# Adding the experts' rows to the nodes: accumulating scatters and per-tile combining in a two-layer graph network on one Trainium2 core

## What is computed

```python
x = x + L0_gnn(layernorm(x), src, dst, ...)      # attention over edges, then a dense FFN
x = x + L0_ffn(layernorm(x), gate_w, gate_b, w1, b1, w2, b2)
x = x + L1_gnn(layernorm(x), edge_attr_4, edge_attr_8, src, dst, ...)
x = x + L1_ffn(layernorm(x), ...)

# L0_ffn: top-2 of 8 experts, at most cap = int(1.2 * T / 8) = 187 rows per expert
topw, topi = top_k(softmax(xf @ gate_w.T + gate_b), 2)
w_te = einsum('tk,tke->te', topw, one_hot(topi)); wm = where(routed, w_te, -1)
sel_w, sel_idx = top_k(wm.T, cap)
h = gelu(xf[sel_idx] @ w1 + b1); out = h @ w2 + b2            # 512 -> 2048 -> 512
of = zeros.at[sel_idx].add(out * sel_w)

# L1_ffn: a shared FFN plus two banks ("sp", "fq") of 8 experts, top-1 each
y = gelu(x2 @ Ws1 + bs1) @ Ws2 + bs2
for bank in (sp, fq):
    slot, gate = route(x2, Wr, br)                            # capacity is never reached here
    y = y + gate * (gelu(buf @ W1 + b1) @ W2 + b2)[slot]      # 512 -> 256 -> 512
```

## Time and profile before

| | |
|---|---|
| median of 3 runs | 1875.65 us (1869.82 to 1876.59) |
| the profiled execution | 1875.17 us |
| its span in the trace | 1873.4 us |
| PE busy | 1594.3 us, 85% |
| DVE, ACT, POOL busy | 959.7, 701.4, 559.6 us |
| mean granted TensorE clock | 0.925 of 2.4 GHz |
| `experts0` / preparation in `messages` / `experts1` | 863 to 1211 us / 1216 to 1267 us / 1699 us to the end |

### The profile page before, as it was taken

How to read it: one execution, slowest core, us unless ns; L and a number is a source line. 1 busy time by engine, 2 the same in 40 slices (tenths; PEclk the granted TensorE clock), 3 DMA queues, 4 the chain that set the end, 5 groups by cost and what they waited for, 6 DMA issues and landing times. The chain is left out here.

```text
span 1873.4 us, 31644 instructions
## 1 busy us (share of the span) xinstructions
PE 1594.3 (85%) x9860; PEld 1167.9 (62%) x9860; DVE 959.7 (51%) x1950; ACT 701.4 (37%) x1610; POOL 559.6 (30%) x638
## 2 busy tenths in 40 slices
PE   1993077999999797897999999858999999898994
PEld 0551045888888455555999999844555555655662
DVE  8330098766766386361000000168999999542233
ACT  0230055555555133443211112154555555441331
POOL 6777601101010121151000000046555555133133
PEclk6997588999999898798999999968999999998997
DMA  9900011011000600557566552075555555619985
GB/s 290 312 11 6 6 43 23 13 23 22 12 11 1 149 12 1 220 142 249 198 229 238 218 196 99 18 216 165 156 158 158 156 156 150 215 37 287 353 268 183
DMA packets 131143, 252.87 MB, mean 135 GB/s; under 512 B 35344, under 2 KB 52596, under 8 KB 126572
## 3 DMA queue, kind: packets, MB, share of 16 engines
q1 hardware_dynamic: 91692, 171.81, 27.6%
q0 software_dynamic: 39360, 79.86, 14.6%
HBM read 196.03 MB, written 55.52 MB: 134 GB/s over the span
## 5 line engine op out<-in xcount | busy, mean ns | idle before, releaser
L1998 PE MATMUL acc<-prod,ohy 128*64 128x256 f32 x1056 | 249.1, 386 | 7.3 <-DVE prod L2116 7.3
L2042 ACT ACTIVATE ohy<-oh,RECS 128x64 f32<-128x64 f32 x704 | 187.0, 336 | 151.6 <-PE acc L1998 151.6
L1998 PEld LDWEIGHTS acc<-prod,ohy 128*64 128x64 f32 x1056 | 138.4, 138 | 131.9 <-issue 69.5
L1975 POOL DMA_INDIRECT rows<-up_dram,idx x176 | 167.0, 949 | 144.3 <-DVE prod L2116 101.2
L272 POOL DMA_INDIRECT rec_dram<-recs,pos x157 | 160.4, 1022 | 59.9 <-issue 48.9
L2001 PE MATMUL acc<-prod,ohy 128*64 128x256 f32 x704 | 177.3, 395 | 0.0
L1752 DVE TENSOR_SCALAR FT<-y_ps,b2T 128x188 f32<-128x188 f32 x32 | 13.2, 413 | 319.2 <-PE y_ps L1701 319.2
L1689 PE MATMUL hid_ps<-FT,W 128*128 128x188 f32 x1024 | 168.1, 326 | 0.7 <-ACT FT L1726 0.7
L2116 DVE TENSOR_TENSOR prod<-w_ps,rows 128x768 f32<-128x768 f32 x176 | 166.3, 945 | 0.0
L1689 PEld LDWEIGHTS hid_ps<-FT,W 128*128 128x128 f32 x1024 | 165.6, 192 | 0.9 <-issue 0.9
L1701 PE MATMUL y_ps<-hid,W 128*128 128x188 f32 x1024 | 164.5, 323 | 0.0
(11 more groups left out here) (380 smaller groups left out, 2638.2 us busy)
## 6 DMA issues: line engine op xcount, KB each, us to landing
W<-in_L_ffn_w SPq DMA_DIRECT2D x16, 4096.0 KB, 15.9
bankW_sp<-in_L_ffn_W_sp SPq DMA_DIRECT2D x2, 4096.0 KB, 23.9
xin<-zeros SPq DMA_DIRECT2D x31, 256.0 KB
h_dram<-h3e SPq DMA_DIRECT2D x22, 256.0 KB, 4.8
h<-h_dram SPq DMA_DIRECT2D x22, 256.0 KB
QF<-q_dram SPq DMA_DIRECT2D x20, 250.0 KB, 4.1
xin_sp<-zeros SPq DMA_DIRECT2D x17, 256.0 KB
xin_fq<-zeros SPq DMA_DIRECT2D x17, 256.0 KB
```

The lines of the kernel that those rows point to most:

```text
L1975: pool.indirect_dma_start(out=rows[:, t, :], out_offset=None, in_=up_dram, in_offset=bass.IndirectOffsetOnAxis(ap=idx[:, par, t:t + 1], ax ...
L1998: upper = lambda m: nc.tensor.matmul(acc[0:HALFB, bank, :].rearrange("p (b c) -> p b c", c=MUL)[:, m:4:3 - m, :], ohs[:, 1 + m, :], pr[:, ...
L2042: last = nc.scalar.activation(ohy[:, t % OHY, i, :], oh[:, par, t, :], ACT.Copy, scale=RECS[:, bass.ds(BATCH * g + t, 1), 4 + i])
```

## The change

**First expert layer.** `X` is stored to a DRAM buffer `x_dense` during `place_choices` (20 DMAs by SP, between its stores of the hidden layer). The rows of `xin0` are 8 elements wider (520 instead of 512) and carry the two weights, the two expert numbers and the node number; unused rows carry a node number from 1250 up, behind the real nodes. In `experts0` DVE reads the number and the weight from the loaded rows, multiplies the transposed result by the weight on its way to `ye`, and POOL adds each half of 94 rows into `x_dense` with an accumulating indirect scatter; each waits until the one before has landed. `yout0`, `slot_out`, `weight` and the 20 gathers are gone: `send_rows` loads `X` back from `x_dense` with 20 plain DMAs on SP, and DVE starts from there. The clearing of 12 blocks of `MSG` moves from ACT to POOL.

**Second expert layer.** The rows of `xin_sp` and `xin_fq` are wider in the same way. At the end of `tail` SP stores `X` to `x_shared` (20 DMAs). In `experts1` every row tile is combined by itself: POOL gathers the 128 nodes' running rows (`x_shared` for the first bank, `x_first` for the second) into a ring of 5, DVE adds the gated result, POOL scatters them on (to `x_first`, or to the output). A gather waits until the scatter five tiles before has landed, the first gather of the second bank until all of the first bank's scatters have. The final gathers, adds and stores are gone. `ye` is a ring of 4 instead of 3.

```diff
-        X = sb("X", [P, TILES, DIM])
+        X128 = sb("X", [128, TILES, DIM])
+        X = X128[0:P]
...
                         for b in range(ECHUNKS):
                             store_hidden(sp, b)
+                            if b < TILES:
+                                for p0, p1 in TILE_PARTS:
+                                    sp.dma_start(x_dense[P * b + p0:P * b + p1, :], X[p0:p1, b, :]).then_inc(x_stored, 16)
...
+                        for e in range(EXPERTS):
+                            b = e % 2
+                            pool.wait_ge(noted, 2 * (e + 1))
+                            for c in range(2):
+                                pool.wait_ge(back_moved, 2 * e + c + 3)
+                                if e + c >= 1:
+                                    pool.wait_ge(landed, 16 * (2 * e + c))
+                                pool.indirect_dma_start(
+                                    out=x_dense, out_offset=bass.IndirectOffsetOnAxis(ap=nodeI[:, e, c:c + 1], axis=0),
+                                    in_=ye[b][:, c, :], in_offset=None, compute_op=ALU.add).then_inc(landed, 16)
+                        pool.wait_ge(landed, 32 * EXPERTS)
...
-                                    nc.vector.tensor_copy(ye[b][:, c, :], turn_ps[:HALF0, c, :]).then_inc(back_moved, 1)
+                                nc.vector.tensor_scalar(ye[b][:, c, :], turn_ps[:HALF0, c, :], weight[:, e, c:c + 1], None, ALU.mult
+                                                        ).then_inc(back_moved, 1)
...
+                for t in range(TILES):
+                    if t == 2:
+                        load_mixer(sp)
+                    for p0, p1 in TILE_PARTS:
+                        sp.dma_start(X[p0:p1, t, :], x_dense[P * t + p0:P * t + p1, :]).then_inc(x_back[t], 16)
...
+                for t in range(TILES):
+                    dve.wait_ge(x_back[t], 32)
+                    step(nc.vector.bn_stats(st6[:, t, :], X[:, t, :]))
+                    nc.vector.bn_aggr(mv[:, t, :], st6[:, t, :]).then_inc(stats_done, 1)
+                    if t >= 1:
                         scale(t - 1)
+                    between(t)
...
                         load_bank(sp)
                         sp.wait_ge(experts_ready, 1)
                         load_biases(sp)
+                        for t in range(TILES):
+                            sp.wait_ge(y_added, t + 1)
+                            for p0, p1 in TILE_PARTS:
+                                sp.dma_start(x_shared[P * t + p0:P * t + p1, :], X[p0:p1, t, :]).then_inc(shared_stored, 16)
...
                             if n >= RING:
                                 sp.wait_ge(x_turned, n - RING + 1)
+                                sp.wait_ge(gates_in, n - RING + 1)
+                                sp.wait_ge(ids_in, n - RING + 1)
...
+                    def combine_step(n):
+                        i = n - TT1
+                        return n + 2 + (0 if i < 0 else max(0, 2 - i // 4))
...
+                        def fetch(n):
+                            pool.wait_ge(ids_in, n + 1)
+                            if n == 0:
+                                pool.wait_ge(shared_stored, 32 * TILES)
                             if n == TT1:
+                                for u in range(FETCHED):
+                                    pool.wait_ge(sent_on[u], 16 * len(range(u, TT1, FETCHED)))
+                            if n >= FETCHED:
+                                pool.wait_ge(sent_on[n % FETCHED], 16 * (n // FETCHED))
+                            pool.indirect_dma_start(
+                                out=got[n % FETCHED], out_offset=None, in_=(x_shared, x_first)[n // TT1],
+                                in_offset=bass.IndirectOffsetOnAxis(ap=nodeI[:, n:n + 1], axis=0)).then_inc(arrived[n % FETCHED], 16)
...
+                        def send_on(n):
+                            pool.wait_ge(weighed, n + 1)
+                            pool.indirect_dma_start(
+                                out=(x_first, result)[n // TT1], out_offset=bass.IndirectOffsetOnAxis(ap=nodeI[:, n:n + 1], axis=0),
+                                in_=got[n % FETCHED], in_offset=None, bounds_check=NODES - 1, oob_is_err=False
+                                ).then_inc(sent_on[n % FETCHED], 16)
...
+                        AHEAD = 3
+                        for first in (0, TT1):
+                            for s in range(TT1 + AHEAD):
+                                if s < TT1:
+                                    fetch(first + s)
+                                if s >= AHEAD:
+                                    send_on(first + s - AHEAD)
...
+                        def weigh(n):
+                            dve.wait_ge(arrived[n % FETCHED], 16 * (n // FETCHED + 1))
+                            dve.wait_ge(y_moved, n + 1)
+                            dve.wait_ge(gates_in, n + 1)
+                            rows = got[n % FETCHED]
+                            nc.vector.scalar_tensor_tensor(out=rows, in0=ye[n % KEPT], scalar=gate[:, n:n + 1], in1=rows,
+                                                           op0=ALU.mult, op1=ALU.add).then_inc(weighed, 1)
...
+                                nc.vector.tensor_copy(nodeI[:, s:s + 1], xe[s % RING][:, DIM + 4:DIM + 5]).then_inc(ids_in, 1)
+                                nc.vector.tensor_copy(gate[:, s:s + 1], xe[s % RING][:, DIM + bank:DIM + bank + 1]).then_inc(gates_in, 1)
```

More of the change, by code:

```diff
@@ L1342, in edge_layers, with place_choices @@
             return on_pe, on_act, store, all_stored
-        def place_choices(N, best, bestI, weight, slot_in, slot_out, sync_work, edges):
+        def place_choices(N, best, bestI, slot_in, sync_work, edges):
             with ExitStack() as st:
@@ L1765, in send_rows @@
+        def send_rows(stack, turn_ps, up_ps):
             sb = tile_in(stack)
-            arrived = sems_in(stack)(*[f"expert_rows{i}" for i in range(RING)])
-            (wup_in, added, stats_done, root_done, steps, scaled, normed, turned, moved, mixed, rows_out, stored) = sems_in(stack)(
-                "wup_in", "added", "ln_stats", "ln_root", "ln_steps", "ln_scaled", "normed", "turned", "turned_moved",
+            x_back = sems_in(stack)(*[f"x_back{t}" for t in range(TILES)])
+            (wup_in, stats_done, root_done, steps, scaled, normed, turned, moved, mixed, rows_out, stored) = sems_in(stack)(
+                "wup_in", "ln_stats", "ln_root", "ln_steps", "ln_scaled", "normed", "turned", "turned_moved",
@@ L1888, in all_out, with messages @@
                 engine.wait_ge(rows_out, TILES)
-            return load, first_added, store, fetch, all_stored, on_pe, on_act, on_dve, all_out
-        def messages(MSG, picks):
+            return load, store, all_stored, on_pe, on_act, on_dve, all_out
+        def messages(MSG):
             BATCH = 8
@@ L2555, in _ @@
                                 load_second(sp, (e, e + 1))
-                        for t in range(TILES):
-                            sp.wait_ge(added, TILES + t + 1)
-                            for p0, p1 in TILE_PARTS:
-                                sp.dma_start(result[P * t + p0:P * t + p1, :], X[p0:p1, t, :]).then_inc(result_stored, 16)
-                        sp.wait_ge(result_stored, 32 * TILES)
-                    def fetch(pool, bank, t, dst, done):
-                        source, slots, _ = picks[bank]
-                        pool.indirect_dma_start(out=dst, out_offset=None, in_=source,
-                                                in_offset=bass.IndirectOffsetOnAxis(ap=slots(t), axis=0)).then_inc(done, 16)
+                    def combine_step(n):
+                        i = n - TT1
+                        return n + 2 + (0 if i < 0 else max(0, 2 - i // 4))
                     @block.gpsimd
@@ L2734, in gnn_moe_gnn_moe @@
             MSG = sb1("MSG", [128, BLOCKS, DIM])
-            messages(MSG, [(yout0, lambda t, c=c: slot_out[:, t, c:c + 1], lambda t, c=c: weight[:, t, c:c + 1]) for c in range(2)])
+            messages(MSG)
             with ExitStack() as ffn:
```

244 lines of the change are left out of this document (101 added, 143 removed).

## The result

The changed kernel takes 1890.3 us (median of 6 runs, 1885.0 to 1895.2), the kernel before beside it 1876.0 (median of 6): **0.9% slower**, ratio 1.0089, interval 1.0073 to 1.0105. The forecast was 1869, "the same", range 1860 to 1884. So the prediction was wrong, in sign and range. Ratios and intervals leave out executions in a second, slower state; one here was in it, of e5, with 2030 us at a granted clock of 0.80.

The account below looks back on a forecast made before the run. Bounds: PE's row-tile chain in experts1, then POOL's gathers, and barriers at stage boundaries; DMA mostly had room. Terms 12.3 - 9.5 + 6.8 + 2.0 + 1.5 - 19.4 = -6.3 on 1875.2 gave 1869 us, range 1860 to 1884.

Parts of the forecast that it names:

- Front, dense, place_choices: Stages ahead of experts0: added fills, wider rows and 20 x_dense stores find room; 0 us.
- End of experts0: Last two accumulating scatters in series, 8.0 us each plus a 1.5 us boundary, in place of 5.2 us; +12.3 us.
- upper bound from a store of both halves: End of experts0: POOL's 188-row store, 11.4 us at best, taken as a scatter landing's upper limit; term's end +19.1.
- estimate by the Trainium skill's rule: End of experts0: 94 rows run on two DMA engines, landing near 10 us; term near +16.
- Preparation: In messages: first apply 2.9 us sooner, nine following intervals gain 6.5 us; -9.5 us, ends -6 and -11.
- End of tail: SP's 20 x_shared stores behind its bias loads delay the barrier and first row load; +6.8 us, ends +5 and +10.
- Start of experts1: First gather waits behind POOL's ten scatters, DVE stands 5 us, some 3 absorbed; +2 us, ends 0 and +5.
- First bank under load: In experts1, 17 gathers add 4.5 MB to loaded DMA, second bank's weights slightly late; +1.5 us.
- starved bank: Rival: in experts1 shared DMA engines bring weights 17.7 us late at row tile 17; 1885 us, chance 0.12.
- The end: After experts1's last bias add only a gated add and one scatter of 4.0 us remain; -19.4 us.
- rival with quick scatters: Accumulating scatters at experts0's end land like plain ones, 4.2 us: 4.7 instead of 12.3, 1861 us; chance 0.24.
- POOL fall behind per row tile: Rival: in experts1 POOL can't hold two indirect DMAs per tile, scatters queue at the end; near 1880, chance 0.04.

Follow-up runs that it names:

- e5: e2 with the first three experts1 gathers issued behind POOL's second, fourth and sixth scatters, not all ten; 1866.3 us beside 1873.1, ratio 0.9958.
- e1: The changed kernel with experts0 scatters that write rows without adding; 1883.2 us, one run.
- e6: e2 with the 20 x_shared stores of tail issued by ACT in place of SP; 1872.5 us beside 1873.1, ratio 1.0003.
- e7: e2 with both edits, the early gathers of e5 and the stores by ACT of e6; 1866.3 us beside 1873.1, ratio 0.9969.
- e9: e5 with eight places for fetched node rows in place of five; 1871.7 us beside 1875.5, ratio 0.9987.
- e10: e7 with eight places for fetched node rows; 1870.3 us beside 1875.5, ratio 0.9981.
- e8: e2 with the last row tile's scatter sent, without bounds check, to a buffer with rows for all numbers; 1879.0 us, one run.
- e2: The changed kernel with experts0 scatters of 96 rows in place of 94, the two more holding zeros; 1874.3 us beside 1873.3, ratio 1.0009.

## Why the prediction was wrong

- **Front, dense, place_choices: 0.** Nothing shows. The -3.9 us ahead lie within the spread of 5.7 us of all profiles.
- **End of experts0: +12.3, measured +24.2.** This is the step that failed. The mechanism was right, two scatters in series, but the landing was mis-sized: I took 8.0 us each, "about the middle", where the last two took 12.2 and 12.7, and the upper bound from a store of both halves (11.4) was no bound. A bound from a plain DMA does not bound an adding one: e1 puts the add at 4.4 us on top of 8.6. That is 8.9 of the 11.9 us. The other 3.0 are steps beside the landings, for which I had 1.5 us and which took 4.5: 0.9 from the half `ye` to POOL's issue, 0.8 from a landing to the next issue, 2.8 from the last landing to the next stage. This term alone is 11.9 of the 19.6 us between forecast (-6.3) and measured spans (+13.3). The estimate by the Trainium skill's rule, near +16, had the cause right, and I put the number in the middle all the same; but its 6.6 us of transfer were some 9, and with it the forecast would have been 1873, still "the same".
- **Preparation: -9.5, measured -9.8.** The sum is right partly by luck. The first apply gained 1.8 us where I had 2.9, and the nine intervals 8.0 where I had 6.5: they took 23.4 us, the kind end. My ends were added wrongly, too: nine intervals of 2.96 are 26.6 us, three of them with six of 2.54 are 24.1, not 26.3 and 23.5.
- **End of tail: +6.8, measured +6.4.** Right in size, with errors that cancel: the twenty issues took 9.26 us and not 7.3, but SP came to them 0.9 us sooner against DVE's add, and 0.5 us behind its last issue the stage was left, not 1.5. The cause was half right: e6 shows that another queue takes the same stores no sooner, so the list of SP is not the whole of it.
- **Start of experts1: +2, measured +8.0.** The place was right. The landing I put at 9.3 us took 12.5, and "some 3 us are absorbed" was 1.0. e5 shows the cause: with the same gathers behind two, four and six scatters, all of it goes.
- **First bank under load: +1.5, measured +2.5** (at the change of bank). In e5, without the hole, 363 GB/s were moved and the eighteenth row tile was as early as before; I had taken 353 to 380. The starved bank, my rival for "slower", did not decide; but the late rows and gathers of e7, e9 and e10 point to it as the next bound.
- **The end: -19.4, measured -13.5.** I let the end come with the landing, 4.0 us after the gated add. Measured are 9.9: 0.8 between add and issue, 0.98 of issue, and 8.1 that POOL takes behind it, for which I had no term. The landing itself was not too short: 2.1 us with no row to write, under 3 in e8 with all 128.
- The rival with quick scatters did not come to pass, nor did POOL fall behind per row tile. e2 makes the scatters as quick as this rival had them (4.1 us), and the stretch is still 12.9 us, not 9.9: the same steps beside the landings.
- In the earlier trace rows two slices near the end are at 9 tenths, not three; nothing hangs on it.

The preparation and the end of tail came out within 0.4 us, though parts of each were off by 1 to 2 us. Of the three terms that missed by 5 us and more, two were landings of POOL's DMAs, taken over from another shape or another load, and one was a time behind POOL's last issue that no row of the kernel before had on its path. These three had one sign. The range of 1860 to 1884 did not hold the upper ends together: +19.1, +5, +6 and -15.7 with the rest as forecast make +11.7, that is 1887, and even this lies below the measured 1890.

## What to carry to other kernels

Before a DMA of rows is put on the path, look at its row count: two rows of padding (94 to 96) were worth 8 us per transfer here, and the DMA share in slices shows at once whether one engine in ten or most of them work. Where gathers feed an in-order engine, issue the first few ahead of bulk scatters on the same queue, as soon as their row numbers are known. And where the last work of a kernel is POOL's indirect DMA, count the 8 us behind its issue that every profile here has, and don't expect a change that shortens the end to give more than that leaves.

## What was not expected of the hardware

- A scatter of 94 rows of 2 KB landed in 12.2 us at best with the add and 7.7 without; with 96 rows and the add in 4.0. POOL's issue took 2.55, 1.47 and 1.42 us.
- The last two scatters of 94 rows and those of 96 rows used the same DMA engine time (8.9% of 16 engines over 35 us), in 1536 packets and in 224; the busy share within a transfer was 0.15 and 0.93.
- The span ended 7.8 to 8.7 us after the issue of POOL's last indirect DMA was over, in fourteen profiles; in e8 that DMA had written its 128 rows within 2.5 us of its issue.
- Stores issued by ACT beside bias loads of SP took a median 0.68 and up to 3.12 us to issue, where SP's took 0.36 and up to 0.87.
